# Cross-attention with keys on the partitions: scores that need no turning, maxima and sums across partitions

## The reference

```python
q = (text_hidden @ Wq)      # 2 x 256 x 16 heads x 128
k = (vision_tokens @ Wk)    # 2 x 4096 x 8 heads x 128, each for two query heads
v = (vision_tokens @ Wv)
scores = einsum('bhtd,bhsd->bhts', q, k) / sqrt(128)
scores = where(mask, scores, -inf)
attn = nan_to_num(softmax(scores, axis=-1), nan=0.0)
out = einsum('bhts,bhsd->bhtd', attn, v)
return out @ Wo
```

## Time and profile before

| | |
|---|---|
| median of 3 runs | 1957.9 us (1955.37 to 1959.71) |
| profiled execution, span from first to last instruction | 1954.8 us |
| what lies around the span, against the median | 3.1 us |
| TensorE busy, share of the span | 1903.1 us, 97% |
| VectorE | 1096.9 us, 56% |
| ScalarE | 977.7 us, 50% |
| GpSimd | 330.1 us, 17% |

### The profile page before, as it was taken

One profiled execution on the slowest core, in us unless ns is written; L12 is line 12 of the kernel. 1 busy time (PEld: TensorE's weight loads), 2 busy tenths in 40 slices (PEclk: granted clock), 3 DMA queues, 4 the chain that ended last, 5 costly groups with the idle time before them and its releaser, 6 DMA issues. The chain is left out here.

```text
span 1954.8 us, 32112 instructions
## 1 busy us (share of the span) xinstructions
PE 1903.1 (97%) x10494; PEld 1595.7 (82%) x10494; DVE 1096.9 (56%) x2447; ACT 977.7 (50%) x2079; POOL 330.1 (17%) x241
## 2 busy tenths in 40 slices
PE   9999999999999989999999999999897999999998
PEld 6787888888888868878888888887765688999997
DVE  3567677677677665676677676676656530000003
ACT  3204676676676573055765775765745441121111
POOL 0300211211211113002112112112552300000001
PEclk9999999999999999999999999999999999999998
DMA  7651111111111146601111111111300907677552
GB/s 245 215 194 44 39 52 41 40 43 40 51 33 38 43 128 199 201 20 52 33 46 48 35 46 46 32 38 43 97 33 23 347 6 268 225 265 263 188 189 67
DMA packets 123281, 198.12 MB, mean 101 GB/s; under 512 B 12741, under 2 KB 62021, under 8 KB 119104
## 3 DMA queue, kind: packets, MB, share of 16 engines
q1 hardware_dynamic: 119040, 188.59, 29.0%
q10 hardware_dynamic: 2880, 4.55, 0.7%
q0 software_dynamic: 1280, 3.93, 0.6%
HBM read 151.50 MB, written 45.81 MB: 101 GB/s over the span
## 5 line engine op out<-in xcount | busy, mean ns | idle before, releaser
L861 DVE TENSOR_TENSOR crs_ptl<-crs_tp,crs_pth 128x512 fp32r<-128x512 f32 x512 | 352.4, 689 | 178.6 <-ACT crs_pth L688 177.9
L688 ACT ACTIVATE crs_pth<-crs_tp 128x512 fp32r<-128x512 f32 x504 | 301.5, 599 | 244.1 <-PE crs_tp L1088 240.8
L606 POOL TENSOR_TENSOR crs_vl<-crs_vraw,crs_vh 128x512 fp32r<-128x512 f32 x128 | 164.9, 1288 | 1070.9 <-ACT crs_vh L695 1070.8
L1079 PE MATMUL crs_ring<-crs_kh,crs_ql 128*128 128x512 f32 x512 | 234.2, 457 | 0.3 <-DVE crs_kl L865 0.3
L1098 PE MATMUL crs_ov<-crs_ptl,crs_vh 128*128 128x512 f32 x512 | 209.5, 409 | 9.2 <-DVE crs_ptl L861 7.0
L1079 PE MATMUL crs_ring<-crs_kh,crs_qh 128*128 128x512 f32 x512 | 202.3, 395 | 0.0
L1098 PE MATMUL crs_ov<-crs_pth,crs_vh 128*128 128x512 f32 x512 | 202.3, 395 | 0.0
L1079 PE MATMUL crs_ring<-crs_kl,crs_qh 128*128 128x512 f32 x512 | 201.4, 393 | 0.0
L1098 PE MATMUL crs_ov<-crs_pth,crs_vl 128*128 128x512 f32 x512 | 199.1, 389 | 0.0
L1088 PEld LDWEIGHTS crs_tp<-all_ident,crs_prob 128*128 128x128 f32 x1024 | 143.0, 140 | 68.7 <-ACT crs_more L677 4.2
L1088 PE MATMUL crs_tp<-all_ident,crs_prob 128*128 128x128 f32 x1024 | 195.2, 272 | 3.4 <-ACT crs_more L677 3.4
(11 more groups left out here) (284 smaller groups left out, 3334.6 us busy)
## 6 DMA issues: line engine op xcount, KB each, us to landing
moe_w<-in_L_ffn_w SPq DMA_DIRECT2D x48, 1024.0 KB, 12.3
v_scratch<-crs_more SPq DMA_DIRECT2D x64, 512.0 KB, 2.9
crs_vraw<-v_scratch SPq DMA_DIRECT2D x128, 256.0 KB, 2.8
ex_w<-in_L_ffn_w SPq DMA_DIRECT2D x16, 1024.0 KB, 13.5
crs_prob<-in_ctx SPq DMA_DIRECT2D x16, 512.0 KB, 4.7
crs_wo<-in_L_xattn_Wo SPq DMA_DIRECT2D x16, 512.0 KB, 4.1
moe_w<-in_L_ffn_sw SPq DMA_DIRECT2D x8, 1024.0 KB, 13.7
qry_wq<-in_L_xattn_Wq SPq DMA_DIRECT2D x16, 256.0 KB, 4.0
```

The source lines that it names most:

```text
L606: nc.gpsimd.tensor_tensor(vl[:, n % VR, :, :], vraw[:, :, :], vh[:, n % VR, :, :].bitcast(F32), ALU.subtract).then_inc(s["v_lo"], 1)
L688: act.activation(pth[:, k % PT, :], tp[k % PT][:, :], ACT.Copy).then_inc(s["pt_hi"], 1)
L861: v.tensor_tensor(ptl[:, k % PT, :], tp[k % PT][:, :], pth[:, k % PT, :].bitcast(F32), ALU.subtract).then_inc(s["pt_lo"], 1)
L1079: m = pe.matmul(ring[at % RING][:, :], a[:, t // RT, rows], w[:, n % KR, :], start=i == 0, stop=i == 2)
```

## The change

Scores are made with the key chunk as the stationary operand and the 512 queries streaming, so that a bank holds 128 keys by 512 queries, the form that values need; nothing is turned. The mask becomes one column per chunk (`maskc`). ScalarE copies scores out with that column as bias (`keep_scores`); VectorE keeps a running maximum of the 32 chunks, partition by partition (`maxima`). At the head of the next group TensorE turns the 128 x 512 maxima, VectorE reduces them and TensorE spreads the negative maxima over all partitions (`nm_ps`); VectorE adds them to two chunks at a time (`less_maximum`) and ScalarE takes exponentials of two chunks (`exponentials`) and copies high parts (`probs_high`). The low parts of the probabilities are GpSimd's (`probs_low`). Sums over keys are float32 matmuls with ones, four chunks into four strips of 32 partitions of one bank (`sum_probs`), and the strips are added at the end (`add_parts`). Both parts of the keys are now VectorE's (`keys_split`). The three `tp` banks go; `nm_ps` and `sums` come; high and low parts have four buffers instead of three.

```diff
-        def score(R, n, t, op): ... for i, (a, w) in enumerate(((ql, kh), (qh, kl), (qh, kh))):
-                    m = pe.matmul(ring[at % RING][:, :], a[:, t // RT, rows], w[:, n % KR, :], ...)
-            def turn(u, k): ... m = pe.transpose(tp[k % PT][:, t * P:(t + 1) * P], probs(t, k * P, (k + 1) * P), ident[:, :])
+            def score(R, k, op):
...
+                for i, (w, a) in enumerate(((kl, qh), (kh, ql), (kh, qh))):
+                    m = pe.matmul(ring[at % RING][:, :], w[:, n % KR, cols], a[:, :, :].rearrange("p h n -> p (h n)"), start=i == 0, stop=i == 2)
+            def turn_maxima(u, R):
+                pe.wait_ge(s["ring_free"], R)
...
+                    m = pe.transpose(nm_ps[:, t * P:(t + 1) * P], mx[:, t * P:(t + 1) * P], ident[:, :])
+            def spread_maxima(u):
...
+                    m = pe.matmul(nm_ps[:, t * P:(t + 1) * P], nmax[:, t:t + 1].to_broadcast([P, P]), ident[:, :], start=True, stop=True)
+            def add_parts(u):
...
+                    m = pe.matmul(sums[:, t:t + 1], parts[:, t * P:(t + 1) * P], part[:, :], start=True, stop=True)
+            def sum_probs(u, n):
+                pe.wait_ge(s["exp_ok"], u * PAIRS + (2 * n + 2))
...
+                for c in range(NC):
+                    m = pe.matmul(sums[c * TILE:(c + 1) * TILE, :], ones[:, :], probs(n * NC + c), start=n == 0, stop=n == SB - 1)
             def pv(u, k):
-                pe.wait_ge(s["pt_lo"], u * SCH + (k + 1))
+                pe.wait_ge(s["p_lo"], u * SCH + (k + 1))
                 if k % NC == 0:
                     pe.wait_ge(s["v_lo"], u * SB + (k // NC + 1))
+            def group(b, u, R, op):            # TensorE
+                turn_maxima(u, R)
+                keys_make(R, 0, op)
+                spread_maxima(u)
+                keys_make(R, 1, op)
+                if op:
+                    add_parts(u - 1)
+                    for t in range(QT):
+                        project(R, o_at(t), t, u - 1)
+                keys_make(R, 2, op)
+                pe.wait_ge(s["q_lo"], q_count(b, u + 1))
+                for n in range(SB):
+                    for t in range(NC):
+                        k = n * NC + t
+                        score(R, k, op)
+                        if t == 1:
+                            sum_probs(u, n)
+                        if k >= LAG:
+                            pv(u, k - LAG)
+                    if n <= SB - 4:
+                        keys_make(R, n + 3, op)
+                for k in range(SCH - LAG, SCH):
+                    pv(u, k)
...
+            def keep_scores(b, R, u, k, op):   # ScalarE
+                act.activation(probs(k), ring[s_at(k, op) % RING][:, :], ACT.Identity, bias=maskc[:, b, k:k + 1]).then_inc(s["kept"], 1)
+            def exponentials(u, i):
+                act.activation(pair(i), pair(i), ACT.Exp).then_inc(s["exp_ok"], 1)
+            def probs_high(u, k, projected=None):
...
+                    act.wait_ge(s["pv_done"], u * SCH + (k - SLOTS + 1))
+                act.activation(ph[:, k % SLOTS, :], probs(k), ACT.Copy).then_inc(s["p_hi"], 1)
+            def begin(u):
+                exponentials(u, 0); probs_high(u, 0); probs_high(u, 1); exponentials(u, 1)
+            def ahead(u, m, projected):
+                exponentials(u, m + 2); probs_high(u, 2 * m + 2, projected); probs_high(u, 2 * m + 3)   # while there are any
+            def group(b, u, R, op, last=False):
+                if op:
+                    outputs_high(u - 1)
+                query_high(u + 1, R)
+                begin(u)
+                for m in range(PAIRS):
+                    keep_scores(b, R, u + 1, 2 * m, op)
+                    keep_scores(b, R, u + 1, 2 * m + 1, op)
+                    ahead(u, m, ...)
+                    # odd m: values_high of the next block; m = 4: output_weight_high
...
+            def keys_split(R, u, n, op):       # VectorE: tensor_copy to kh, then the subtraction to kl
+            def maxima(b, R, u, k, op):
+                v.wait_ge(s["kept"], u * SCH + (k + 1))
...
+                    v.wait_ge(s["ring_free"], R + (s_at(k - 1, op) + 1))
+                    m = v.scalar_tensor_tensor(mx[:, :], bank[:, :], maskc[:, b, k:k + 1], mx[:, :], ALU.add, ALU.max)
+            def maximum(u):
+                v.tensor_reduce(nmax[:, :], nm_ps[:, :].rearrange("p (t k) -> p t k", t=QT), op=ALU.max, axis=AX.X, negate=True).then_inc(s["less_ok"], 1)
+            def less_maximum(u, i):
+                v.tensor_tensor(pair(i), pair(i), nm_ps[:, :].rearrange("p (o n) -> p o n", o=1).to_broadcast([P, 2, BANK]), ALU.add).then_inc(s["less_ok"], 1)
+            def group(b, u, R, op):
+                maximum(u)
+                if op:
+                    output_low(u - 1)
+                keys_split(R, u + 1, 0, op); less_maximum(u, 0); keys_split(R, u + 1, 1, op); less_maximum(u, 1)
+                if op:
+                    inverse(u - 1)
+                    for t in range(QT):
+                        residual(b, R, o_at(t), t, u - 1)
+                query_low(b, u + 1)
+                keys_split(R, u + 1, 2, op); less_maximum(u, 2)
+                for m in range(PAIRS):
+                    maxima(2 * m); less_maximum(u, m + 3); maxima(2 * m + 1); # odd m: keys_split
...
+            def probs_low(u, k):               # GpSimd
+                pool.wait_ge(s["p_hi"], u * SCH + (k + 1))
+                nc.gpsimd.tensor_tensor(pl[:, k % SLOTS, :], probs(k), ph[:, k % SLOTS, :].bitcast(F32), ALU.subtract).then_inc(s["p_lo"], 1)
+            def block_low(u, n):
+                for k in range(n * NC + 2, min(n * NC + NC + 2, SCH)):
+                    probs_low(u, k)
             u = G - 1                          # the last unit
-            for n in range(SB - 1):
-                values_low(u, n + 1)
+            probs_low(u, 0)
+            probs_low(u, 1)
+            for n in range(SB):
+                block_low(u, n)
+                if n < SB - 1:
+                    values_low(u, n + 1)
                 if n == 2:
                     output_low(u)
-                if n >= 3:
+                if 3 <= n < SB - 1:
...
+                    weight_part(pool, prob, w_hi, w_lo, w, half, s["aw_ok"], s["aw_ok"], 2 * (n - 3) + 1)
```

More of the change, by code:

```diff
@@ L433, in v_out @@
             return v_pair(n)[:, :, n % 2, :]
-        mask_u8 = [more[:, r, 4 * BANK:5 * BANK].bitcast(U8) for r in range(2)]
         def wv_part(ring, quad, c):
@@ L500, in values_load @@
             def values_load(b, j, n, u):
-                if not (isinstance(u, int) and u == 0 and n == 0):
+                if not (is_first(u) and n == 0):
                     sp.wait_ge(s["v_lo"], u * SB + n)
@@ L521, in _ @@
                 if b == 0:
-                    for r in range(2):
-                        sp.dma_start(mask_u8[r], mask[b:b + 1, r * (S // 2):(r + 1) * (S // 2)].to_broadcast([P, S // 2])).then_inc(s["mask_ld"], 16)
+                    sp.dma_start(mask_u8[:, :, :], mask).then_inc(s["mask_ld"], 16)
                     keys_weight(0)
@@ L1009, in group @@
-                if pv:
-                    inverse(u)
-                    for t in range(NC):
-                        scores_out(R, SB - 1, t, op)
-                maxima(R, op)
+                        maxima(b, R, u + 1, n * NC + t, op)
+                    if n <= SB - 4:
+                        keys_split(R, u + 1, n + 3, op)
+                    if op and n == SB - 2:
+                        ln_deviation(v, ch, norm, 0, RT, s["root_ready"], 1)
+            def group(b, u, R, op):
+                maximum(u)
+                if op:
+                    output_low(u - 1)
+                keys_split(R, u + 1, 0, op)
+                less_maximum(u, 0)
+                keys_split(R, u + 1, 1, op)
+                less_maximum(u, 1)
+                if op:
+                    inverse(u - 1)
+                    for t in range(QT):
+                        residual(b, R, o_at(t), t, u - 1)
+                query_low(b, u + 1)
+                keys_split(R, u + 1, 2, op)
+                less_maximum(u, 2)
+                for m in range(PAIRS):
+                    n = m // 2
+                    maxima(b, R, u + 1, 2 * m, op)
+                    if m + 3 < PAIRS:
+                        less_maximum(u, m + 3)
+                    maxima(b, R, u + 1, 2 * m + 1, op)
+                    if m % 2 and n <= SB - 4:
+                        keys_split(R, u + 1, n + 3, op)
+                    if m == 2:
+                        some_valid(u)
@@ L1017, in _ @@
                 first_part(b)
-                group(b, u0 - 1, ring_base(b, 0), b > 0, False)
-                group(b, u0, ring_base(b, 1), False, True)
+                scores_alone(b, u0 - 1, ring_base(b, 0), b > 0)
+                group(b, u0, ring_base(b, 1), False)
                 with v.Fori(2, HKV) as g:
-                    group(b, g + (u0 - 1), ring_base(b, g), True, True)
```

(22 more changed lines are left out.)

507 lines of the change are left out of this document (213 added, 294 removed).

## The result

The changed kernel takes 2248.05 us (median of 4 runs, 2245.75 to 2248.66) against 1956.63 for the one before on the same chip: a ratio of 1.1487, 95% interval 1.1467 to 1.1506. The forecast was 2003, its range 1948 to 2065: the direction was right, the time lies 183 us above the range.

The account below looks back on a forecast made before the run. TensorE's queue bounds the kernel, 97% busy. Groups +8, scores alone +4, between batches +3.5 and last unit +30 make +45.5 on the profiled 1954.8, so 2000; with 3.1 around the span, 2003 us, range 1948 to 2065.

Parts of the forecast that it names:

- The wait inside the group: Steady group: V's low part, queued behind GpSimd's four low parts, makes values wait 1.1 us behind blocks 5 and 6.
- TensorE's sum of 69.1: Steady group: TensorE's work after the change, in us; alone it would win 3.2 us per group.
- The waits of 2.2 and 1.6: Steady group, us: TensorE waits 2.2 for V's low part and 1.6 at the head for the query.
- Scores alone: Stages making only scores: each maximum waits for the one ahead; 36.7 instead of 32.64 us, both stages together +4.
- Sums side by side: Probability sums on TensorE: four float32 matmuls overlap, 0.89 us plus 0.31 for shape changes; eight sums are 9.6.
- Rival 2: Probability sums on TensorE run in sequence: 2.66 us more, 128 times, giving 2312; chance 0.04.
- VectorE and GpSimd beside each other: Groups: GpSimd's low parts keep 1.29 us beside VectorE's maxima, if the mask column does not count as an SBUF input.
- rival 3: Groups: VectorE and GpSimd hold each other up, +7 to +17 us in 14 groups, some 2100 to 2240; chance 0.09.
- Between the batches and the last unit: Two stages: +3.5 us between batches as GpSimd sets the pace; last unit 82.5 against 52.6, GpSimd 65 in a row.
- Rival 1: Groups: TensorE keeps its bound at 69.1 us per group, kernel faster: 1951, or 1916 with free shape changes; chance 0.16.
- the prediction's own signs of being wrong: Groups falling to 69 us, low parts or maxima lengthening, or a last unit under 65 us.

Follow-up runs that it names:

- both rings cut: The changed kernel with exponentials and high parts ahead of ScalarE's score copies and VectorE's subtraction for pair m + 3 ahead of both maxima: 2053.66 us, 1.0489.

## Why the prediction was wrong

By its own steps:

1. *The wait inside the group: failed, and it carries nearly the whole miss.* The prediction followed one chain, from score 4n+3 by "0.2 until ScalarE starts, 0.58 to its next start" to V's low part. ScalarE does not start 0.2 behind the score. It starts when the low part of the old chunk in that place is done, a wait which the change adds and which stands in `keep_scores`. The chain was laid as a line that begins at a score; it is a ring, and its length over 16 pairs is the group's time. Cutting it, with the one that takes its place, brought the groups from 1253.7 to 1060.2 us: 193 of the 245 between forecast and result. That each engine's sum fits was right and says nothing about a ring.
2. *TensorE's sum of 69.1: 3 too low.* With both rings cut it is busy for 72.2. From start to start, idle time taken off, a group's 252 matmuls of 512 columns take 63.0 us instead of 57.1, the sums 8.0 instead of 9.6 (the changes of shape, put into the sums, lengthen the matmuls ahead and behind), the small ones 2.0 instead of 2.4; 0.8 of this are short gaps that count as idle. The prediction took every such matmul at the undisturbed pace of 0.227. Unbroken, scores and values take 0.695 for three, 0.232 each, which is some 1.3 us per group; and the first matmul behind a wait or a change of shape starts the next one 0.1 later than others do. The rest was not followed. Together with idle time of 3.8 a group is 76.0, not 72.9: 14 times 3.1 is 43 more of the miss. So TensorE's work was in truth not less than before (72.28).
3. *The waits of 2.2 and 1.6: the sum came out by luck.* The idle time is 3.8 with both rings cut, but of the terms only the query's is there, at 1.0 instead of 1.6, the first score 11.43 us behind the turn (predicted 10.9). V's low part is not late then; the waits for maxima and residuals, which the prediction left out, fill its place.
4. *Scores alone: mis-sized.* Each maximum was taken at 0.74 + 0.035 behind the one ahead; starts are 0.85 apart (10.15 for 12). 36.7 became 39.2. (The text's +4 for these stages is also 1.6 short of its own terms: 2 x 4.06, less 2 x 2.5, and 2.5.) Two running maxima showed that this wait is the cause in the first batch; in the second ScalarE's table loads stand beside it.
5. *Sums side by side: right.* Four stand in one round of 0.996 us; with the 0.1 that is lost ahead of them and the 0.1 behind, 1.2, as taken. Rival 2 is out. Rows of after, by form:

```profile
L843 DVE SCALAR_TENSOR_TENSOR crs_mx<-crs_ring,crs_maskc,crs_mx 128x512 f32<-128x512 f32 x496 | 371.3, 749 | 433.9 <-ACT crs_more L657 272.3 <-ACT crs_prob L657 156.5
L600 POOL TENSOR_TENSOR crs_pl<-crs_prob,crs_ph 128x512 fp32r<-128x512 f32 x256 | 327.4, 1299 | 328.4 <-ACT crs_ph L671 328.3
...
L1103 PE MATMUL crs_sums<-crs_prob,crs_ones 128*32 128x512 f32 x512 | 138.1, 618 | 42.7 <-ACT crs_more L661 42.5
```

6. *VectorE and GpSimd beside each other: right for this kernel.* Low parts took 1.30 and maxima 0.749, as their nearest rows had it, so rival 3 is out. The contention is real where both inputs of VectorE lie in SBUF, as with the weights (a GpSimd pair 3.96 instead of 2.5) and the early query. The Trainium skill (SBUF — State Buffer, "Who interferes with whom") says so; these rows agree, and they add that a column of 128 values beside one full SBUF input and a PSUM bank did not count.
7. *Between the batches and the last unit: right.* 139.0 for 138.3 and 83.9 for 82.5, with GpSimd busy for 65.07 in the last unit (predicted 65); moving the weights showed that its series is the bound.

Rival 1, TensorE as the only bound, was not reached by any order tried. The other side of the range was too near because no rival let the engines wait for each other in a ring. That the measured time lies next to the 2100 to 2240 of rival 3 is chance, as step 6 shows its condition not met. Nor would the prediction's own signs of being wrong have told: it named shorter groups, longer low parts or maxima and a shorter last unit, and none of these came.

## What to carry to other kernels

When a change writes new data over old in place, list the wait that this adds and follow it until it comes back to its own instruction: the time round the ring, over the steps it covers, is a lower bound that no sum of busy times shows. In a table of waits the longest on the bound engine may be only the last link; look for rows in which two engines each wait for the other. An edit of order can close one ring as it opens another, so try the orders of both engines alone and together.

## What was not expected of the hardware

- A VectorE maximum that waits for the one just ahead of it starts 0.85 us behind it, for a record of 0.749; where it waits for the one before that, starts were 0.70 apart, the pace of ScalarE's copies.
- Behind an idle time of some 2.4 us TensorE's granted clock fell to the lower level (0.50) in nine of twelve heads with the query early, for some 3 us, and stayed at 1.00 in three.
- A VectorE subtraction of 128x512 with both inputs in SBUF took 1.39 us beside a GpSimd low part and 0.68 without; the join of the two maxima, also of two SBUF inputs, took 1.53 while GpSimd made low parts.
- Four float32 matmuls with 32 columns each, in four strips of one bank, took 0.996 us together, not much over the 0.89 of one by the earlier trace rows.
